# The first attention stage of a long fused kernel: its two ends reordered, and TensorE given forty transposes of the identity ahead of its first scores

## The chip, the cores and the metric

The kernel runs on one core of one Trainium2 chip. The metric is the device time of one launch in microseconds, as the median of several runs. The engines are called by their short names: PE (TensorE), DVE (VectorE), ACT (ScalarE), POOL (GpSimd) and SP (SyncE, which here only issues DMAs).

## The reference, cut to what matters

Four layers follow each other, each of the form `x = x + layernorm(f(layernorm(x)))` on eight batches of 512 x 512 float32:

```
x = x + _layernorm(_L0_attn_ref(_layernorm(x)))            # this case: its start and its end
x = x + _layernorm(_L0_ffn_ref(_layernorm(x), factors, bias))   # one matrix, the sum of 8 factors
x = x + _layernorm(_L1_attn_ref(_layernorm(x), ...))       # 8 heads, 2 groups
x = x + _layernorm(_L1_ffn_ref(_layernorm(x), ...))        # gated, 1408 wide

def _L0_attn_ref(x):
    scores = jnp.einsum('bci,bcj->bij', x, x)
    weights = jax.nn.softmax(scores, axis=-1)
    return jnp.einsum('bij,bcj->bci', weights, x)
```

The input of the kernel also holds `x_t`, the input turned, from which the context's right operand comes.

## The kernel before

**Precision.** Every float32 operand of a product is split into a high part (`xh`, `xth`, `pth`: the value written as fp32r) and a low part (`xl`, `xtl`, `ptl`: what is left), and a product is three matmuls: high by high, low by high, high by low. So the 512 x 512 scores of a batch take, for each of four row tiles `t`, three matmuls for each of four `k`. The scores are symmetric: row tile `t` computes only its columns from `t` on, and gets the rest by transposing what earlier tiles left (`copy_upper` on ACT puts it into `upper`, PE turns it back in line 901).

**The stage.** `attention_and_map` holds the first attention layer and, interleaved behind it, the first map. Each engine has its own instruction list, written out by hand for batches 0 to 7 (`written_out(body)`), and semaphores tie the lists together; within an engine the order is the order of the list, so an instruction that waits holds all behind it. For one batch:

- SP loads `x` (1 MB) and `x_t` in two halves (`load_half`, which waits until DVE has made the low parts of the batch before); for batch 0 the four tiles of `x` come in four DMAs.
- DVE takes row statistics (`tile_stats`, line 616; aggregated in 623 or 631), POOL turns them into `rs` and `shift` (`first_scales`, `scales_of`, the helper `row_scales` in lines 104 to 109), ACT writes the high part `xh` (`hi_of_xn`, line 444), POOL writes `x_scaled = x * rs` (`scaled_x`, line 315), and DVE writes the low part `xl = x_scaled + shift - xh` (`lo_of_xn`, line 637). For batch 0 this is done in two halves of two tiles.
- PE makes the scores (`scores`, line 907) in two PSUM banks; DVE takes the maximum (`maximum`, 650), ACT the exponential (`exp`, 455), DVE the inverse of the row sum (`inverse`, 655), POOL the division (`probabilities`, 320), PE turns the result (`turn`, 917), ACT and DVE split it (`hi_of_prob` 468, `lo_of_prob` 660), and PE makes the contexts (`contexts`, line 58) from it and `xth`, `xtl` (464, 643). The contexts of batch b-1 lie between the scores of batch b.
- DVE takes the contexts' statistics (`output_stats`, 665), POOL the scales (`output_scales`), ACT the normalization (`norm`, 476), and POOL adds to `x` (`add`, 336).
- POOL also issues the DMAs that sum the eight factors of the next layer's matrix (`add_factor`, 343), each waiting until the one before it has landed.

**Where scores wait.** Before the first tile of any batch but 0, PE waits for all four tiles of `xh` and `xl` of that batch; for batch 0 it waits tile by tile, one `k` at a time:

```
if t == 0 and not first:
    pe.wait_ge(xh_ready, (b + 1) * T)
    pe.wait_ge(xl_ready, (b + 1) * T)
...
    if first and t == 0:
        pe.wait_ge(xl_ready, k + 1)
```

**The end of the stage.** In the last batch's list DVE has, between `lo_of_prob(7, 1)` and `inverse(7, 3)`, the four tile statistics and their aggregation of batch 1's map. After its list ACT has `norm(6, 2)` and `norm(6, 3)` and then the high parts of the map's first turned tiles (`map_hi(0, 0, t)`, line 496), which DVE needs for the low parts (`map_lo`, 697). PE's order there is `turn(7, 2)`, `turn(7, 3)`, `contexts(6, 3)`, `map_turn` 0 and 1 (line 959), `contexts(7, 0)`, `map_turn` 2, `contexts(7, 1)`, `map_turn` 3, `contexts(7, 2)`, `contexts(7, 3)`. `map_turn` 2 waits for `map_lo` 0, whose bank it takes.

Of the kernel before, what the change touches and what calls it, by code (L numbers as in the profile page):

```python
# [15 lines left out]
T = N // P  # L16
# [14 lines left out]
ALU = mybir.AluOpType  # L31
# [47 lines left out]
def written_out(body):  # L79

    for b in range(B):
        body(b, b % 2, b == 0, b == B - 1)
# [60 lines left out]
def attention_and_map(nc, s, resident, x_in, xt_in, factors, bias, x_out, attention_buffers, following):  # L143


    if True:
# [94 lines left out]
        def block_at(t):  # L241
            return slice(t * P, (t + 1) * P)
# [50 lines left out]
        def _(pool):  # L293
# [11 lines left out]
                           pool_step, b * 2 + 2).then_inc(scales, 1)  # L305

            def scaled_x(b, tiles):
                if b == 0:
                    pool.wait_ge(*((first_scaled, 1) if tiles[0] == 0 else (scales, 1)))
                elif tiles[0] == 0:  # L310
                    pool.wait_ge(scales, b + 1)
                for t in tiles:
                    if b > 0:
                        pool.wait_ge(xl_ready, (b - 1) * T + t + 1)
                    nc.gpsimd.tensor_scalar(x_scaled[:, t, :], s.x[:, b * T + t, :], rs[:, t:t + 1], 1.0,
                                            ALU.mult, ALU.mult).then_inc(scaled_ready, 1)

# [44 lines left out]

            for h in range(2):
                first_scales(h)
                scaled_x(0, (2 * h, 2 * h + 1))

            def body(b, p, first, last):
                if not last and not first:
# [67 lines left out]
        def _(act):  # L436
# [33 lines left out]
            def norm(b, t):  # L470
                act.wait_ge(oscales, b * 2 + t // 2 + 1)
                if b == B - 1 and t >= 4:
                    act.wait_ge(last_added, t - 4 + 1)
                elif b * T + t >= 4:
                    act.wait_ge(added, b * T + t - 4 + 1)
                nc.scalar.activation(normed[:, t % 4, :], context[t][:, :], ACT.Identity,
                                     bias=oshift[:, t:t + 1], scale=ors[:, t:t + 1]).then_inc(ctx_normed, 1)
# [12 lines left out]
            def map_hi(b, p, t):  # L490
                act.wait_ge(m_turn_ready, b * T + t + 1)
                if t == 0 and b == 1:
                    act.wait_ge(ctx_ready, (B - 1) * T)
                if t == 0 and b >= 2:
                    act.wait_ge(mix_ready, (b - 1) * T)
                nc.scalar.copy(m_xth[p][:, :, block_at(t)], blocks_of(m_turned[t % 2][:, :])).then_inc(m_hi_ready, 1)
# [67 lines left out]
                    hi_of_prob(b, p, 3)  # L564

            written_out(body)
            norm(B - 2, 2)
            norm(B - 2, 3)
            map_hi(0, 0, 0)
            map_hi(0, 0, 1)  # L570
            map_hi(0, 0, 2)
            map_hi(0, 0, 3)
            norm(B - 1, 0)
# [36 lines left out]
        def _(dve):  # L610
# [47 lines left out]
            def lo_of_prob(b, p, g):  # L658
                dve.wait_ge(hi_ready, b * T + g + 1)
                nc.vector.tensor_tensor(ptl[p][:, :, block_at(g)], blocks_of(turned[g % 2][:, :]),  # L660
                                        pth[p][:, :, block_at(g)].bitcast(F32), ALU.subtract).then_inc(lo_ready, 1)
# [61 lines left out]
            for h in range(2):  # L723
                tile_stats(0, 2 * h)
                tile_stats(0, 2 * h + 1)
                first_stats_of(h)
            for t in range(T):
                lo_of_xn(0, 0, t)

            def body(b, p, first, last):  # L730
                if b >= 2:
# [43 lines left out]
                    lo_of_xn(1, 1, 2)  # L775
                maximum(b, p, 3)
                lo_of_prob(b, p, 1)
                if last:
                    for t in range(T):
                        map_tile_stats(1, t)  # L780
                    map_stats(1)
                elif first:
                    lo_of_xn(1, 1, 3)
                else:
                    lo_of_xn(b + 1, 1 - p, 2)
                inverse(b, p, 3)
                if not last and not first:
                    lo_of_xn(b + 1, 1 - p, 3)
                if not first:
# [100 lines left out]
        @block.tensor  # L890
        def _(pe):
            def scores(b, p, t, first):
                if t == 0 and not first:
                    pe.wait_ge(xh_ready, (b + 1) * T)
                    pe.wait_ge(xl_ready, (b + 1) * T)
                if not (first and t < 2):
                    pe.wait_ge(exp_ready, b * T + t - 1)
                if t > 0:
                    pe.wait_ge(copied, b * (T - 1) + t)
                for r in range(t):  # L900
                    nc.tensor.transpose(score[t % 2][:, block_at(r)], upper[r][:, block_at(t - r - 1)],
                                        s.identity[:, :])
                for k in range(T):
                    if first and t == 0:
                        pe.wait_ge(xl_ready, k + 1)
                    for l, r in ((xh, xh), (xl, xh), (xh, xl)):
                        own = nc.tensor.matmul(score[t % 2][:, t * P:], l[p][:, k, block_at(t)], r[p][:, k, t * P:],  # L907
                                               start=(k == 0 and l is xh and r is xh),
                                               stop=(k == T - 1 and r is xl))
                own.then_inc(scored, 1)  # L910
# [52 lines left out]
            def mixes(b, p, t):  # L963
# [6 lines left out]
                if b > 0:  # L970
# [2 lines left out]
                         [(l[p][:, k, block_at(t)], r[:, k, :])  # L973
                          for k in range(T) for l, r in ((m_xth, mh), (m_xtl, mh), (m_xth, ml))]).then_inc(mix_ready, 1)

            written_out(body)
            map_turn(0, 0, 0)
            map_turn(0, 0, 1)
# [1533 lines left out]
```

## Time and profile before

| | us |
|---|---|
| median of 3 runs (lowest to highest) | 1439.12 (1436.91 to 1440.38) |
| the profiled execution | 1436.28 |
| its span | 1434.5 |
| PE busy in the span | 1378.0 |
| mean granted clock of PE, as a share of full speed | 0.994 |

The first attention stage is the stretch from 0 to about 197 us. A profile of an execution gives for every instruction its start and its duration, and for an engine that stood idle before it the instruction that released it. PE's matmuls are pipelined: a matmul's duration is longer than the distance to the next one, and it is the distance that counts.

### The profile page before, as it was taken

How to read it: one execution, taken by the hardware profiler on the slowest of the kernel's cores; microseconds unless marked ns; L12 is line 12 of the kernel's file. 1: busy time of each engine (PE TensorE's matmuls, PEld its weight loads, DVE VectorE, ACT ScalarE, POOL GpSimd, SP SyncE). 2: the span in 40 equal slices, each digit the busy share in tenths (PEclk: the TensorE clock that was granted, in tenths of full speed). 3: DMA queues.
4: the chain of work that ended last, by engine and by line, in shares of the span. 5: the costliest groups of instructions: out<-in, count | busy, mean ns of one | idle time of the engine just before them, and what ended most of it. 6: DMA issues, size and time to landing. Idle time of an engine off the chain costs nothing.

```text
span 1434.5 us, 20717 instructions
## 1 busy us (share of the span) xinstructions
PE 1378.0 (96%) x6864; PEld 1131.6 (79%) x6864; DVE 1008.4 (70%) x2070; ACT 797.2 (56%) x1554; POOL 739.3 (52%) x1008
## 2 busy tenths in 40 slices
PE   5999999988999999999999998899999999999996
PEld 4888877866788888888888887688888888888884
DVE  5888868978999998989899989565343342524433
ACT  4666746649787778787878787542132222213221
POOL 5788646656547464656555555553332424333241
PEclk9999999999999999999999999999999999999998
DMA  6665232341203121221212140440101001010100
GB/s 202 166 168 122 57 103 89 118 132 45 89 16 98 36 66 53 59 74 38 89 37 89 37 141 2 147 140 1 59 1 59 31 27 58 0 58 0 58 30 30
DMA packets 53516, 101.32 MB, mean 71 GB/s; under 512 B 3760, under 2 KB 4784, under 8 KB 53424
## 3 DMA queue, kind: packets, MB, share of 16 engines
q1 hardware_dynamic: 49728, 92.83, 19.5%
q0 software_dynamic: 3696, 7.34, 3.1%
q8 instruction: 49, 0.80, 0.2%
q14 instruction: 43, 0.35, 0.1%
HBM read 70.79 MB, written 25.17 MB: 67 GB/s over the span
## 4 chain that ended last, share of the span: by engine, by line
PE 78%; DVE 11%; ACT 4%; POOL 3%; issue 3%; DMA 1%; DVEq 0%; POOLq 0%; SPq 0%; ACTq 0%
PE context L1915 12%; PE score L2393 11%; PE context L2393 11%; PE context L58 7%; PE score L58 6%; PE context L2421 5%; PE turned L2421 5%; PE score L907 4%; PE turned L1951 4%; PE context L1977 3%; PE context L1979 3%; PE context L1951 2%; DVE g_neg_max L1775 1%; DVE g_ptl L1794 1%; DVE g_q L1692 1%
## 5 line engine op out<-in xcount | busy, mean ns | idle before, releaser
L1422 POOL TENSOR_SCALAR g_prob<-g_prob,g_inv_sum 128x512 f32<-128x512 f32 x256 | 178.2, 698 | 247.3 <-DVE g_inv_sum L1780 247.3
L1560 ACT ACTIVATE g_prob<-score,g_neg_max 128x512 f32<-128x512 f32 x256 | 177.4, 693 | 105.0 <-DVE g_neg_max L1775 102.1
L2169 POOL TENSOR_TENSOR f_hl<-f_hidden,f_hh 128x512 fp32r<-128x512 f32 x88 | 121.9, 1386 | 215.8 <-DVE f_hh L2302 215.8
L1775 DVE TENSOR_REDUCE g_neg_max<-score 128x1 f32<-128x512 f32 x256 | 174.2, 680 | 30.3 <-PE score L58 29.6
L2393 PE MATMUL context<-g_hth,f_w 128*128 128x512 f32 x352 | 137.7, 391 | 2.2 <-ACT f_w L2219 2.1
L2393 PE MATMUL score<-g_hth,f_w 128*128 128x512 f32 x352 | 137.8, 392 | 0.6 <-DVE g_htl L2319 0.5
L2393 PE MATMUL context<-g_htl,f_w 128*128 128x512 f32 x352 | 137.1, 390 | 0.0
L2393 PE MATMUL score<-g_htl,f_w 128*128 128x512 f32 x352 | 137.1, 390 | 0.0
L58 PE MATMUL score<-g_kh,g_q 128*128 128x512 f32 x256 | 122.9, 480 | 7.7 <-ACT g_prob L1560 5.9
L2225 ACT ACTIVATE f_silu<-score,g_bits 128x512 f32<-128x512 f32 x44 | 30.4, 690 | 176.1 <-PE score L2393 176.1
L2225 ACT ACTIVATE f_silu<-context,g_bits 128x512 f32<-128x512 f32 x44 | 30.4, 691 | 174.4 <-PE context L2393 174.4
L2293 DVE SCALAR_TENSOR_TENSOR f_hidden<-score,g_bits,f_silu 128x512 f32<-128x512 f32 x44 | 33.0, 750 | 131.3 <-PE score L2393 131.3
L2293 DVE SCALAR_TENSOR_TENSOR f_hidden<-context,g_bits,f_silu 128x512 f32<-128x512 f32 x44 | 33.0, 749 | 128.5 <-PE context L2393 128.5
L1794 DVE TENSOR_TENSOR g_ptl<-turned,g_pth 128x512 fp32r<-128x512 f32 x171 | 115.9, 678 | 10.3 <-ACT g_pth L1607 8.9
L1607 ACT CAST g_pth<-turned 128x512 fp32r<-128x512 f32 x171 | 100.0, 585 | 12.2 <-PE turned L1951 10.5
L1951 PE MATMUL turned<-identity,g_prob 128*128 128x128 f32 x684 | 102.3, 272 | 4.0 <-POOL g_prob L1422 3.9
L1977 PE MATMUL context<-g_pth,g_v 128*128 128x512 f32 x256 | 101.3, 396 | 3.0 <-DVE g_out_sum L1728 2.8
L1951 PEld LDWEIGHTS turned<-identity,g_prob 128*128 128x128 f32 x684 | 84.1, 140 | 25.2 <-POOL g_prob L1422 5.3
L58 PE MATMUL score<-g_kl,g_q 128*128 128x512 f32 x256 | 100.9, 394 | 0.0
L1979 PE MATMUL context<-g_ptl,g_v 128*128 128x512 f32 x256 | 100.7, 393 | 0.0
L2393 PEld LDWEIGHTS context<-g_hth,f_w 128*128 128x128 f32 x352 | 66.1, 188 | 17.8 <-ACT f_w L2219 2.5
L2393 PEld LDWEIGHTS score<-g_hth,f_w 128*128 128x128 f32 x352 | 66.1, 188 | 16.2 <-DVE g_htl L2319 2.3
(261 smaller groups left out, 3941.7 us busy)
## 6 DMA issues: line engine op xcount, KB each, us to landing
xt<-x_t SPq DMA_DIRECT2D x16, 512.0 KB, 5.9
x_mixed<-x_resident SPq DMA_DIRECT2D x8, 1024.0 KB, 4.8
x_pair<-x_mixed SPq DMA_DIRECT2D x8, 1024.0 KB, 7.6
g_res<-x_mixed SPq DMA_DIRECT2D x8, 1024.0 KB, 6.2
x_attended<-g_res SPq DMA_DIRECT2D x8, 1024.0 KB, 5.1
x_pair<-x_attended SPq DMA_DIRECT2D x8, 1024.0 KB, 5.6
x_resident<-x SPq DMA_DIRECT2D x7, 1024.0 KB, 10.0
factor_sum<-factors POOLq DMA_DIRECT2D x7, 1024.0 KB, 10.9
```

Of the source, the lines that this page charges most:

```text
L58: last = nc.tensor.matmul(out, lhsT, rhs, start=(n == 0), stop=(n == len(pairs) - 1))
L1422: nc.gpsimd.tensor_scalar(prob[:, at, :], prob[:, at, :], inv_sum[:, at:at + 1], 1.0, ALU.mult, ALU.mult).then_inc(prob_ready, 1)
L1560: nc.scalar.activation(prob[:, at, :], score[u % 2][:, :], ACT.Exp, bias=neg_max[:, at:at + 1], scale=1.0, accum_out=row_sum[:, at:at + 1] ...
L1775: nc.vector.reduce_max(neg_max[:, at:at + 1], score[u % 2][:, :], AX, negate=True).then_inc(max_ready, 1)
L1794: nc.vector.tensor_tensor(ptl[:, at, :, cols], blocks_of(turned[(g - TURN_LAG) % 3][:, :]), pth[:, at, :, cols].bitcast(F32), ALU.subtract ...
L1915: last = nc.tensor.matmul(out[:, :], *pairs[n], start=(k == 0 and n == 0), stop=(k == T - 1 and n == 2))
L1951: mm = nc.tensor.transpose(turned[(g - TURN_LAG) % 3][:, cols], prob[:, turn_u % 4, cols], s.identity[:, :])
L1977: nc.tensor.matmul(output[:, :], lhsT, pth[:, hd % 2, t, :], start=(t == 0), stop=False)
L1979: mm = nc.tensor.matmul(output[:, :], lhsT, ptl[:, hd % 2, t, :], start=False, stop=(t == T - 1))
L2169: self.nc.gpsimd.tensor_tensor(self.hl[:, at, :], self.hidden[:, at, :], self.hh[:, at, :].bitcast(F32), ALU.subtract).then_inc(self.hl_re ...
L2393: last = self.nc.tensor.matmul(self.inner[pair_at(p, i) + j][:, :], lhsT, rhs, start=(k == 0 and n == 0), stop=(k == T - 1 and n == len(pa ...
L2421: last = self.nc.tensor.matmul(self.down[t][:, :], l, r, start=(i == 0 and n == 0), stop=(i == IT - 1 and n == len(halves) - 1))
```

## The change

In batch 0 the multiplication `x * rs` goes from POOL to DVE, half by half in front of the low parts. PE's wait for the inputs of a batch's first scores goes tile by tile for every batch. At the end of the stage DVE takes `inverse(7, 3)` ahead of the map statistics, and ACT takes `map_hi` 0 and 1 ahead of `norm(6, 2)` and `norm(6, 3)`. PE's list begins with forty transposes of the identity into the PSUM bank `context[3]`, which nothing reads until `contexts(0, 3)` has written it.

```diff
--- before.py
+++ after.py
@@ -305,13 +305,10 @@
                            pool_step, b * 2 + 2).then_inc(scales, 1)
 
             def scaled_x(b, tiles):
-                if b == 0:
-                    pool.wait_ge(*((first_scaled, 1) if tiles[0] == 0 else (scales, 1)))
-                elif tiles[0] == 0:
+                if tiles[0] == 0:
                     pool.wait_ge(scales, b + 1)
                 for t in tiles:
-                    if b > 0:
-                        pool.wait_ge(xl_ready, (b - 1) * T + t + 1)
+                    pool.wait_ge(xl_ready, (b - 1) * T + t + 1)
                     nc.gpsimd.tensor_scalar(x_scaled[:, t, :], s.x[:, b * T + t, :], rs[:, t:t + 1], 1.0,
                                             ALU.mult, ALU.mult).then_inc(scaled_ready, 1)
 
@@ -362,7 +359,6 @@
 
             for h in range(2):
                 first_scales(h)
-                scaled_x(0, (2 * h, 2 * h + 1))
 
             def body(b, p, first, last):
                 if not last and not first:
@@ -564,10 +560,10 @@
                     hi_of_prob(b, p, 3)
 
             written_out(body)
+            map_hi(0, 0, 0)
+            map_hi(0, 0, 1)
             norm(B - 2, 2)
             norm(B - 2, 3)
-            map_hi(0, 0, 0)
-            map_hi(0, 0, 1)
             map_hi(0, 0, 2)
             map_hi(0, 0, 3)
             norm(B - 1, 0)
@@ -724,8 +720,16 @@
                 tile_stats(0, 2 * h)
                 tile_stats(0, 2 * h + 1)
                 first_stats_of(h)
-            for t in range(T):
-                lo_of_xn(0, 0, t)
+            def first_scaled_x(h):
+                dve.wait_ge(*((first_scaled, 1) if h == 0 else (scales, 1)))
+                for t in (2 * h, 2 * h + 1):
+                    nc.vector.tensor_scalar(x_scaled[:, t, :], s.x[:, t, :], rs[:, t:t + 1], 1.0,
+                                            ALU.mult, ALU.mult).then_inc(scaled_ready, 1)
+
+            for h in range(2):
+                first_scaled_x(h)
+                lo_of_xn(0, 0, 2 * h)
+                lo_of_xn(0, 0, 2 * h + 1)
 
             def body(b, p, first, last):
                 if b >= 2:
@@ -775,15 +779,15 @@
                     lo_of_xn(1, 1, 2)
                 maximum(b, p, 3)
                 lo_of_prob(b, p, 1)
+                if first:
+                    lo_of_xn(1, 1, 3)
+                elif not last:
+                    lo_of_xn(b + 1, 1 - p, 2)
+                inverse(b, p, 3)
                 if last:
                     for t in range(T):
                         map_tile_stats(1, t)
                     map_stats(1)
-                elif first:
-                    lo_of_xn(1, 1, 3)
-                else:
-                    lo_of_xn(b + 1, 1 - p, 2)
-                inverse(b, p, 3)
                 if not last and not first:
                     lo_of_xn(b + 1, 1 - p, 3)
                 if not first:
@@ -890,9 +894,6 @@
         @block.tensor
         def _(pe):
             def scores(b, p, t, first):
-                if t == 0 and not first:
-                    pe.wait_ge(xh_ready, (b + 1) * T)
-                    pe.wait_ge(xl_ready, (b + 1) * T)
                 if not (first and t < 2):
                     pe.wait_ge(exp_ready, b * T + t - 1)
                 if t > 0:
@@ -901,8 +902,8 @@
                     nc.tensor.transpose(score[t % 2][:, block_at(r)], upper[r][:, block_at(t - r - 1)],
                                         s.identity[:, :])
                 for k in range(T):
-                    if first and t == 0:
-                        pe.wait_ge(xl_ready, k + 1)
+                    if t == 0:
+                        pe.wait_ge(xl_ready, b * T + k + 1)
                     for l, r in ((xh, xh), (xl, xh), (xh, xl)):
                         own = nc.tensor.matmul(score[t % 2][:, t * P:], l[p][:, k, block_at(t)], r[p][:, k, t * P:],
                                                start=(k == 0 and l is xh and r is xh),
@@ -973,6 +974,8 @@
                          [(l[p][:, k, block_at(t)], r[:, k, :])
                           for k in range(T) for l, r in ((m_xth, mh), (m_xtl, mh), (m_xth, ml))]).then_inc(mix_ready, 1)
 
+            for i in range(40):
+                nc.tensor.transpose(context[3][:, block_at(i % T)], s.identity[:, :], s.identity[:, :])
             written_out(body)
             map_turn(0, 0, 0)
             map_turn(0, 0, 1)
```

## Rows read from the trace of the kernel before

**Rows 1.** The page: busy time of PE, its share of the span, instructions.

```profile
PE 1378.0 (96%) x6864; PEld 1131.6 (79%) x6864; DVE 1008.4 (70%) x2070; ACT 797.2 (56%) x1554; POOL 739.3 (52%) x1008
```

**Rows 2.** Windows: stretch, length, busy PE, PEld, DVE, ACT, POOL, granted clock, DMA.

```profile
25.00:30.00 5.00, 1.45 (x6) 1.13 (x7) 4.64 (x9) 4.09 (x10) 3.86 (x4) 0.75 0.43 96
30.00:35.00 5.00, 5.00 (x18) 3.85 (x17) 2.17 (x4) 1.07 (x4) 0.85 (x1) 0.57 1.10 211
```

**Rows 3.** Waits of PE from 0 to 320 us: total, times, longest.

```profile
PE score L907 <- DVE xl L637: 11.3, 2, 10.1
PE score L907 <- issue: 3.5, 1, 3.5
PE turned L917 <- POOL prob L320: 1.9, 1, 1.9
...
PE score L959 <- DVE xl L697: 1.7, 1, 1.7
```

**Rows 4.** Timeline, 8 to 18 us: start, duration of all, engine, line, instruction.

```profile
8.18 1.37 POOL L315 TENSOR_SCALAR x_scaled<-x_resident,rs 128x512 f32<-128x512 f32 x2
8.42 0.25 DVE L623 BATCH_NORM_AGGREGATE mv<-bn 128x2 f32<-128x6 f32 x2
...
12.23 1.52 ACT L444 ACTIVATE xh<-x_resident,shift,rs 128x512 fp32r<-128x512 f32 x2 [2.61 <-POOL shift L109]
...
13.15 1.72 DVE L637 SCALAR_TENSOR_TENSOR xl<-x_scaled,shift,xh 128x512 fp32r<-128x512 f32 x2 [2.41 <-ACT xh L444]
...
14.69 1.14 ACT L464 CAST xth<-xt 128x512 fp32r<-128x512 f32 x2 [0.93 <-DMA xt<-x_t]
...
17.23 0.48 ACT L449 COPY upper<-score 128x384 f32<-128x384 f32 x1 [1.40 <-PE score L907]
```

**Rows 5.** The chain of waits, 0 to 240 us: start, length, engine, line.

```profile
14.27 2.94 PE score L907 x6
...
29.09 5.41 PE score L907 x12
...
52.97 2.76 PE score L907 x12
```

**Rows 6.** Groups of DVE: busy us, mean ns of one, idle before.

```profile
L2302 DVE CAST f_hh<-f_hidden 128x512 fp32r<-128x512 f32 x88 | 38.1, 433 | 15.2 <-PE turned L2421 6.4 <-DVE f_hidden L2293 0.9
```

**Rows 7.** Timeline, 174 to 188 us, the end of the stage.

```profile
175.15 2.47 DVE L683 BATCH_NORM_STATS2 m_bn<-x_resident 128x6 f32<-128x512 f32 x4
...
178.66 2.52 DVE L643 TENSOR_TENSOR xtl<-xt,xth 128x512 fp32r<-128x512 f32 x2
181.10 1.27 DVE L660 TENSOR_TENSOR ptl<-turned,pth 128x512 fp32r<-128x512 f32 x2
...
178.24 0.70 POOL L320 TENSOR_SCALAR prob<-prob,inv_sum 128x512 f32<-128x512 f32 x1 [3.89 <-DVE inv_sum L655]
...
183.08 0.48 PE L58 MATMUL context<-pth,xth 128*128 128x512 f32 x1
...
186.37 1.07 ACT L496 CAST xh<-score 128x512 fp32r<-128x512 f32 x2
```

**Rows 8.** Timeline, 28 to 59 us, DVE, POOL and PE.

```profile
28.25 0.73 DVE L637 SCALAR_TENSOR_TENSOR xl<-x_scaled,shift,xh 128x512 fp32r<-128x512 f32 x1
...
29.17 1.68 POOL L320 TENSOR_SCALAR prob<-prob,inv_sum 128x512 f32<-128x512 f32 x1 [1.14 <-DVE inv_sum L655]
36.59 1.32 POOL L343 DMA_DIRECT2D factor_sum<-factors  x1 [5.73 <-DMA factor_sum<-factors]
39.17 0.69 POOL L320 TENSOR_SCALAR prob<-prob,inv_sum 128x512 f32<-128x512 f32 x1 [1.26 <-DVE inv_sum L655]
...
34.34 1.04 PE L917 MATMUL turned<-identity,prob 128*128 128x128 f32 x8
...
58.66 0.39 PE L58 MATMUL context<-pth,xth 128*128 128x512 f32 x1
...
56.82 1.29 DVE L660 TENSOR_TENSOR ptl<-turned,pth 128x512 fp32r<-128x512 f32 x2 [1.07 <-ACT pth L468]
```

## The prediction

> **What bounds the kernel now.** I read the page first: PE is busy for 1378.0 of 1434.5 us [rows 1], so what counts is where PE stands idle or runs slowly, and a cut elsewhere is worth something only if a PE wait hangs on it. The windows then give the slow places. The stretch 30 to 35 us has PE busy throughout at a granted clock of 0.57, and the stretch before it has PE busy for 1.45 of 5 us at 0.75 [rows 2]: PE stood idle, the clock fell from the upper to the lower of its two levels (2.4 and 1.2 GHz), and the work after the gap paid for it. The waits of PE in the first attention stage are four kinds that matter: 11.3 us for `xl` of batch 0 (10.1 before the first matmul, 1.2 in the middle), 3.5 us put down to "issue", 1.9 us for `prob` and 1.7 us for the map's low part [rows 3]. The 3.5 us end at 29.09, right after the fourth `xl` of batch 1 (28.25 + 0.73 = 28.98), so they are the wait for all four tiles. Otherwise PE runs through, so a saving ahead of or inside the stage should move all behind it.
>
> **Part 1, batch 0's front.** Now: DVE is free of statistics at 8.67; POOL multiplies until 9.55 and only then makes the second half's scales, which release ACT at 12.23; DVE's low parts start at 13.15; the last six matmuls of score tile 0 follow, ACT's copy starts at 17.23 [rows 4]. The six take 2.94 us from 14.27 [rows 5].
> After: DVE has two multiplications more per half. The trace has none on DVE; the nearest is its cast of a 128x512 float32 tile from one source, 433 ns [rows 6]. The bounds are that and the 0.73 us of one of its low parts (the row at 28.25 [rows 8]); I take 0.4, since one source is what the cast has too. So 8.67 + 0.8 + 0.75 gives the first `xl` at about 10.3 (now 10.1; 10.8 at the other bound). POOL, free of 1.4 us of work, starts the second scales at 8.77 and needs between 1.8 us (alone) and 2.6 us (9.63 to 12.23, beside DVE's low parts): 10.6 to 11.4, and I take 11.0. Then 0.8 + 1.4 us on DVE: last `xl` at 13.3, tile 0 finished at 14.2 at the upper clock, 15.7 at the lower.
> But ACT's list has the casts of `xt` ahead of the copy. They wait for a DMA until 14.69 and end at 15.83 [rows 4], and nothing here moves that DMA. So the copy comes at 15.8 instead of 17.23: **1.4 us**, with up to 1.6 us of work ahead of it hidden. DVE has the four statistics of batch 1 (2.5 us, as for the like row of [rows 7]) ready by 16.1, in time for the maximum.
>
> **Part 2, forty transposes.** PE sits idle until 10.1, and the list starts near 2. In the trace eight transposes take 1.04 us at the upper clock, 0.11 each in sequence [rows 8]. At the lower clock the twelve matmuls of a first score tile take 5.41 us against 2.76 [rows 5], so I double: 0.22 each, 8.8 us, ending near 10.7. If the clock rises on the way they end by 9. The bounds are 0.11 (4.4 us) and 0.28 (11.2 us). At 10.7 they may hold the first matmul by 0.4 us, which the 15.8 of ACT covers. Their worth is the clock: tile 0's matmuls run at 2.94 / 6 = 0.49 us each, the lower level's pace (5.41 / 12 = 0.45), until ACT's copy. That is also hidden by ACT's 15.8, but score tile 1, now begun at 17.8 at the upper clock, would begin at 16.3, perhaps before the clock rises by itself. So the transposes insure rather than add.
> The Trainium skill (TensorE: Matmul & The Clock Gate, Part 4) says that transposes do not count as PE being busy and do not bring the full clock. No stretch of this trace consists of transposes alone, so it neither agrees nor contradicts. What that would make of the time stands among the rivals.
>
> **Part 3, batch 1's scores tile by tile.** With everything 1.4 us earlier, `xl` of batch 1 comes at about 22.9, 23.9, 25.7 and 27.5 (28.98 - 1.4, and the three before it in DVE's list). PE is free at 24.1 and follows them: three matmuls each, the last three done at 28.4. Before, the twelve ended at 34.50 (29.09 + 5.41). PE's gaps are then at most 1.2 us each, and gaps of 1.9 and 1.7 us [rows 3] left the clock alone elsewhere in the stage, so it stays up. `turn(0, 3)` needs the last `prob` of batch 0, ended at 30.85 on POOL (29.17 + 1.68), now 29.4. After it score tile 1 starts at 29.9 instead of 35.2 (34.34 + 0.87): 5.3 us earlier. The next join, `contexts(0, 0)`, needs DVE's low parts at 32.1, when PE arrives as well. **5.3 us in all so far**, of which 2.65 are the clock (5.41 - 2.76).
>
> **Part 4, what is late next.** POOL's second factor DMA waits for the first to land: it sat idle 5.73 us for it and issued at 36.59 [rows 8]. That landing moves only by the 1.4 us of Part 1, to 35.2, so POOL goes on to `prob` of batch 1 at 36.5. Without the hold it would be 39.17 - 5.3 = 33.9. So POOL, and behind it `scales_of(2)`, ACT's `xh`, and DVE's low parts, run 2.6 us behind PE. PE meets them at `contexts(1, 0)`, now at 58.66, which follows DVE's `ptl` (56.82 + 1.29 = 58.11, and 1.07 idle before it). So DVE may be 0.55 + 1.07 = 1.6 us later; it will be some 2.3 (2.6 less 0.3 idle it has on the way). PE loses 0.7. **Front: 5.3 - 0.7 = 4.6 us.** Bounds: 5.3 if the slack holds it all, 4.3 if the whole 2.6 reaches DVE. Per-tile waits help here also: batch 2's tiles come singly.
>
> **Part 5, the stage's end.** `inverse(7, 3)` goes ahead of five statistics operations: it can start at 175.2 instead of 178.0, POOL's `prob` ends at 176.1 instead of 178.94 [rows 7], and PE, through with `turn(7, 2)` only at 177.1, goes straight on: the 1.87 us are gone. PE then wants `contexts(7, 0)` at 183.08 - 1.87 = 181.2, which needs DVE's last `ptl`, ended at 182.37. DVE's list isn't shorter, it is 0.15 longer. But its two `xtl` took 2.52 us where two take 1.29 elsewhere, beside POOL's additions, which now start 2.8 us sooner and are over when the `xtl` begin. That gives 1.2 back: DVE ends at 181.2 to 182.5, and I take 181.3, a wait of 0.1 (bound 1.2).
> With `map_hi` ahead of the two norms, ACT makes it when `map_turn` is done, near 181, instead of 186.37; `map_lo` 0 is there by 183, and PE wants it at 184.2: the 1.73 us are gone. The norms wait for POOL's scales anyway, which come no later, and PE wants `norm(6, 2)` only for `contexts(7, 2)`, 3 us on. **End: 1.87 + 1.73 - 0.1 = 3.5 us** (bounds 2.4 and 3.6). From there to the map's DVE work everything hangs on `contexts(7, 3)` and moves with it; SP's loads for the next layer do too, as they wait for the same contexts.
>
> **Sum.** 4.6 + 3.5 = 8.1 us of the profiled 1436.28: 1428.2. The median of the runs shown is 1439.12, 2.8 above that execution; from the median it is **1431.0**.
>
> **Rivals.**
> *The transposes don't raise the clock.* For: nothing here shows that they do. Score tile 0 then ends at 16.0 (10.7 + 12 x 0.44), 0.2 late, and tile 1's twelve matmuls, 2.1 us at the upper clock, cost between nothing and 1.8 more, as the clock comes up. 8.1 - 0.2 - 0.9 = 7.0: 1432.1. The rule of the Trainium skill (TensorE: Matmul & The Clock Gate, Part 4) would lead here.
> *The clock falls anyway between 24 and 29 us*, PE being idle near half of it. Price up to the 2.65 us of the clock, less what PE would have waited for `turn(0, 3)` (0.6): 6.0 left, 1433.1. Against: the two gaps of nearly 2 us elsewhere.
> *The gain is given back*, because a later hold (POOL's chain of factor DMAs, or the map's DVE-bound stretch) does not move. Against: the waits behind hang on things that move. Then 0 to 2.9 us remain: 1438.
> *Slower: the transposes hold PE.* If one costs more at the lower clock than the doubling says, the first scores are late and everything with them. Up to 0.28 each nothing is lost (11.2 us after 2, then twelve at 0.22 end at 15.8). It takes 8.1 / 40 more, 0.48 each, to eat the gain, and 0.56 to be 2.9 us slower: 1442. Against: 0.56 is five times the 0.11 of the rows, where the clock only doubles.
>
> **How the numbers follow.** A difference of 0.2% (2.9 us) is about what a measurement can tell from none. Chances: forecast 0.50, no higher clock from the transposes 0.28, clock falls anyway 0.08, given back 0.09, slower 0.05. The first three are faster by over 0.2%; with a tenth of the given-back case on that side and 0.02 of the last within 0.2%, that is 0.87, 0.10 and 0.03. The range: front 5.3 and end 3.6 give 8.9, and the runs lie up to 2.2 below their median, of which I take 1.7: 1428.5. At the other side front 4.6 - 1.9 and end 2.4 leave 5.1, and 1.5 for the runs: 1435.5. That leaves out the last two cases and a little more.
>
> **What the profile after would show.** First matmul of scores at 10.3 to 10.8, and 0.22 or 0.43 us to the next; ACT's first copy at 15.8; PE's idle before batch 1's scores in pieces under 1.3 us and no granted clock below 1.00 until the end; POOL's second factor issue near 35.2; a PE wait of some 0.7 us at `contexts(1, 0)`; `turn(7, 3)` right behind `turn(7, 2)`; no wait before `map_turn` 2. The prediction is wrong if the clock column falls again near 27 us, if PE's first scores come after 13 us, or if PE waits at `contexts(7, 0)` for over 1 us.

## The result, and the profile after

The changed kernel takes 1431.41 us (median of 6 runs, 1429.95 to 1433.23), the kernel before 1439.57 (6 runs, 1436.91 to 1440.50): a ratio of 0.9946, 95% interval 0.9933 to 0.9958, or 8.2 us less. The forecast was 1431.0 with 1428.5 to 1435.5. The profiled execution of the changed kernel took 1429.95, its span is 1428.1; against the one of before that is only 6.3 us, and the reason is told below.

The page after, its rows of busy time and of the granted clock:

```profile
PE 1382.8 (97%) x6904; PEld 1136.4 (80%) x6904; DVE 1008.8 (71%) x2074; ACT 796.7 (56%) x1554; POOL 736.3 (52%) x1004
...
PEclk9999999999999999999999999999999999999998
```

PE has 4.8 us more work than in [rows 1], the forty transposes among it, and the span is 6.4 us shorter. The transposes stand in the timeline as one run, at the end of which PE waits for `xl`:

```profile
1.91 7.19 PE L978 MATMUL context<-identity 128*128 128x128 f32 x40 [1.91 <-PEq L1003]
10.21 0.50 PE L908 MATMUL score<-xh 128*128 128x512 f32 x1 [1.11 <-DVE xl L633]
```

The windows after, with the same columns as [rows 2]:

```profile
25.00:30.00 5.00, 4.22 (x23) 3.16 (x22) 4.98 (x10) 4.36 (x10) 3.68 (x3) 1.00 0.39 55
30.00:35.00 5.00, 5.00 (x29) 4.41 (x28) 4.66 (x13) 1.86 (x6) 0.00 (x0) 1.00 1.09 235
```

From 25 to 35 us PE is busy for 9.2 of 10 us at 1.00, where [rows 2] had 6.5 at 0.75 and 0.57. The waits of PE from 0 to 320 us, beside [rows 3]:

```profile
PE score L908 <- DVE xl L633: 2.3, 3, 1.1
PE score L902 <- ACT upper L445: 2.1, 3, 1.0
...
PE turned L918 <- POOL prob L317: 1.8, 3, 1.1
...
PE context L58 <- issue: 0.8, 1, 0.8
```

The 3.5 us and the 1.7 us are gone, and of the 11.3 us for `xl` 2.3 are left, mostly because the transposes now fill the idle time up to 9.10. What is left for `prob` is in the first batch (three waits, the longest 1.1), not at the stage's end. The waits for ACT's copies have grown to 2.1 us; before they were

```profile
PE score L901 <- ACT upper L449: 1.1, 2, 0.6
```

New is 0.8 us of "issue" before a context. The timeline of the front, beside [rows 4] and [rows 8]:

```profile
8.47 0.91 DVE L726 TENSOR_SCALAR x_scaled<-x_resident,rs 128x512 f32<-128x512 f32 x2 [0.43 <-POOL shift L109]
...
11.04 0.89 DVE L726 TENSOR_SCALAR x_scaled<-x_resident,rs 128x512 f32<-128x512 f32 x2 [0.20 <-POOL shift L109]
...
11.04 1.52 ACT L440 ACTIVATE xh<-x_resident,shift,rs 128x512 fp32r<-128x512 f32 x2 [1.05 <-POOL shift L109]
13.84 1.14 ACT L460 CAST xth<-xt 128x512 fp32r<-128x512 f32 x2 [1.27 <-DMA xt<-x_t]
14.88 0.47 ACT L445 COPY upper<-score 128x384 f32<-128x384 f32 x1
...
36.03 1.32 POOL L340 DMA_DIRECT2D factor_sum<-factors  x1 [7.33 <-DMA factor_sum<-factors]
...
51.46 0.30 PE L902 MATMUL score<-identity,upper 128*128 128x128 f32 x1 [0.56 <-ACT upper L445]
...
54.65 0.47 PE L58 MATMUL context<-pth,xth 128*128 128x512 f32 x1 [0.80 <-issue]
```

ACT's first copy comes at 14.88 (forecast 15.8), right behind the casts of `xt`. Of the 2.35 us that it is earlier than in [rows 4], 0.85 aren't the change's: the DMA of `xt` was issued at 7.34 in this execution and let ACT start at 13.84, where the execution of before has 8.11 and 14.69 (and the second trace of the changed kernel, below, 8.11 and 14.92). POOL waits 7.33 us for the first factor DMA and issues the second at 36.03 (forecast 35.2), and PE waits 0.80 before `contexts(1, 0)` (forecast 0.7) and 0.56 at 51.46. The end of the stage, beside [rows 7]:

```profile
174.90 1.28 DVE L639 TENSOR_TENSOR xtl<-xt,xth 128x512 fp32r<-128x512 f32 x2
176.09 1.28 DVE L656 TENSOR_TENSOR ptl<-turned,pth 128x512 fp32r<-128x512 f32 x2
...
176.99 1.08 ACT L492 CAST xh<-score 128x512 fp32r<-128x512 f32 x2 [1.61 <-PE score L960]
179.83 1.45 ACT L472 ACTIVATE normed<-context,oshift,ors 128x512 f32<-128x512 f32 x2 [1.76 <-POOL oshift L328]
...
171.63 0.70 POOL L317 TENSOR_SCALAR prob<-prob,inv_sum 128x512 f32<-128x512 f32 x1 [1.13 <-DVE inv_sum L651]
172.29 2.54 POOL L333 TENSOR_TENSOR x_resident<-x_resident,normed 128x512 f32<-128x512 f32 x2
...
172.67 1.03 PE L918 MATMUL turned<-identity,prob 128*128 128x128 f32 x8
...
176.35 1.04 PE L960 MATMUL score<-identity,x_scaled 128*128 128x128 f32 x8
...
180.32 0.60 PE L960 MATMUL score<-identity,x_scaled 128*128 128x128 f32 x4
```

The two additions of POOL stood later and took longer before:

```profile
178.90 3.44 POOL L336 TENSOR_TENSOR x_resident<-x_resident,normed 128x512 f32<-128x512 f32 x2
```

`turn(7, 2)` and `turn(7, 3)` are one run of eight transposes, `map_turn` 0 and 1 follow twelve matmuls later, ACT makes `map_hi` at 176.99 ahead of the norms at 179.83, and `map_turn` 2 has no wait.

### The profile page after: what moved, and what is told of

It is laid out like the page before. It is cut to its first block, busy times and chain, and to the rows that moved or that the text cites. A ratio compares the mean times of both kernels' runs of the same rounds, so it can differ in the third digit from the quotient of the medians.

```text
span 1428.1 us, 20797 instructions
## 1 busy us (share of the span) xinstructions
PE 1382.8 (97%) x6904; PEld 1136.4 (80%) x6904; DVE 1008.8 (71%) x2074; ACT 796.7 (56%) x1554; POOL 736.3 (52%) x1004
## 3 DMA queue, kind: packets, MB, share of 16 engines
q0 software_dynamic: 3696, 7.34, 3.1%
## 4 chain that ended last, share of the span: by engine, by line
PE 76%; DVE 11%; POOL 4%; ACT 4%; issue 3%; DMA 2%; DVEq 0%; POOLq 0%; SPq 0%; ACTq 0%
PE context L1918 12%; PE score L2396 11%; PE context L2396 11%; PE score L58 6%; PE context L58 6%; PE context L2424 5%; PE turned L2424 5%; PE turned L1954 4%; PE score L908 3%; PE context L1980 3%; PE context L1982 3%; PE context L1954 2%; DVE g_neg_max L1778 1%; DVE g_ptl L1797 1%; DVE g_q L1695 1%
```

## The experiments

Each of the twelve was timed against the kernel before on the same chip, in three groups on three chips, where the median of before was 1439.3 to 1439.9; so the ratio is what to compare. The table has the median, the ratio to before with its interval, and, from one profiled execution each, when PE starts the first matmul of `contexts(0, 0)`, `contexts(1, 0)` and `contexts(7, 1)`. The difference to the first line is what PE has won by then.

| kernel | median | ratio (95%) | contexts(0, 0) | contexts(1, 0) | contexts(7, 1) |
|---|---|---|---|---|---|
| before | 1439.57 | | 37.43 | 58.66 | 188.21 |
| after | 1431.41 | 0.9946 (0.9933 to 0.9958) | 31.48 | 54.65 | 180.67 |
| after_again | 1431.65 | 0.9951 (0.9936 to 0.9966) | 32.76 | 54.55 | 180.43 |
| a_no_turns | 1430.54 | 0.9930 (0.9916 to 0.9944) | 32.32 | 55.35 | 181.21 |
| b_old_end | 1436.87 | 0.9977 (0.9968 to 0.9986) | 32.33 | 56.70 | 187.88 |
| c_whole_wait | 1432.95 | 0.9958 (0.9944 to 0.9971) | 36.14 | 57.37 | 183.23 |
| d_factor_late | 1430.27 | 0.9930 (0.9916 to 0.9943) | 33.45 | 55.45 | 181.39 |
| e_turns_alone | 1438.15 | 0.9992 (0.9982 to 1.0003) | 37.47 | 58.70 | 188.18 |
| f_tiles_alone | 1435.91 | 0.9978 (0.9967 to 0.9988) | 33.66 | 55.16 | 184.78 |
| h_inv_alone | 1437.56 | 0.9993 (0.9983 to 1.0004) | 37.00 | 58.23 | 186.34 |
| k_pool_scaled | 1432.11 | 0.9950 (0.9937 to 0.9964) | 33.57 | 55.27 | 181.16 |
| m_turns60 | 1430.79 | 0.9944 (0.9931 to 0.9958) | 32.11 | 55.75 | 181.61 |
| n_factor_later | 1431.64 | 0.9935 (0.9921 to 0.9948) | 31.87 | 53.08 | 180.42 |
| o_later_no_turns | 1429.29 | 0.9931 (0.9917 to 0.9944) | 32.18 | 53.39 | 179.36 |

The ratios resolve some 2 us. The three time columns resolve tenths, but of one execution: between the two traces of the changed kernel `contexts(0, 0)` differs by 1.3 us, `contexts(1, 0)` by 0.1 and `contexts(7, 1)` by 0.2. Where ratio and trace differ both are told.

**The changed kernel without its transposes** (a_no_turns).

```diff
-            for i in range(40):
-                nc.tensor.transpose(context[3][:, block_at(i % T)], s.identity[:, :], s.identity[:, :])
```

> The changed kernel without the forty transposes. Theory (the start of batch 2 is set by POOL's wait for the first factor DMA, not by PE): score tile 0 runs at 0.43 us a matmul and its copy comes some 0.7 us later, PE's later stretches may be late by up to 1.8 us more, but the hold at contexts(1, 0) takes 1.9 us of whatever the front has, so the whole loses 0 to 0.7 us against the changed kernel: ratio to before about 0.995. Rival 1 (the transposes' clock is worth its full price): 2.5 us lost, ratio 0.9963. Rival 2 (without them the clock never settles before 35 us): 4 us lost, ratio 0.9973.

0.9930, no slower than the changed kernel. In the traces PE is 0.7 to 0.8 us later at `contexts(1, 0)` than in the two of the changed kernel. Both rivals fall (2.5 and 4 us lost); what the transposes give is at most those 0.7 to 0.8 us, at the edge of what the theory allowed. Against the first trace even the 0.7 is the lateness of POOL's second factor issue (36.73 for 36.03), and whether the transposes had a part in that isn't shown.

**The old end with the new front** (b_old_end): the two reorderings of the last hunks for ACT and DVE undone.

```diff
-            map_hi(0, 0, 0)
-            map_hi(0, 0, 1)
             norm(B - 2, 2)
             norm(B - 2, 3)
+            map_hi(0, 0, 0)
+            map_hi(0, 0, 1)
...
-                inverse(b, p, 3)
                 if last:
...
                     map_stats(1)
+                inverse(b, p, 3)
```

> The changed kernel with the end of the stage as before (ACT's two norms ahead of map_hi, DVE's inverse behind the map statistics): the front alone. Theory: the end is worth 3.5 us, so the ratio to before is 0.9946 + 3.5/1439.6 = 0.9970, with waits of 1.9 us for prob and 1.7 us for the map's low part back in the trace. Rival (the end's gain overlaps with something later that waits anyway): 0 to 1.5 us lost, ratio 0.9946 to 0.9957.

0.9977: 4.5 us lost, one more than the order of the work explains, though the intervals allow 3.5. The front of this execution is also poorer (1.96 us won at `contexts(1, 0)`; the first factor landed 11.7 us after its issue at 26.36). But the windows of this execution show something more, in the very stretch of the old end's waits:

```profile
175.00:177.00 2.00, 0.22 (x3) 0.00 (x0) 1.90 (x9) 1.84 (x4) 0.66 (x2) 1.00 0.00 0
177.00:181.00 4.00, 3.91 (x12) 3.28 (x13) 3.45 (x4) 0.59 (x1) 3.40 (x3) 0.57 0.00 0
181.00:183.00 2.00, 2.00 (x14) 1.75 (x13) 0.81 (x3) 0.00 (x0) 0.00 (x0) 1.00 0.00 0
```

PE idle for most of two microseconds, then the clock at 0.57: between `turn(7, 2)`, ahead of the old end's first wait, and `contexts(7, 1)` the gain falls from 1.90 to 0.33 us. In the one execution of before the same wait left the clock at 1.00.

**PE waits for all four tiles again** (c_whole_wait).

```diff
             def scores(b, p, t, first):
+                if t == 0 and not first:
+                    pe.wait_ge(xh_ready, (b + 1) * T)
+                    pe.wait_ge(xl_ready, (b + 1) * T)
...
-                    if t == 0:
-                        pe.wait_ge(xl_ready, b * T + k + 1)
+                    if first and t == 0:
+                        pe.wait_ge(xl_ready, k + 1)
```

> The changed kernel with PE waiting for all four tiles before batch 1's scores and those of later batches. PE then starts batch 1's twelve matmuls near 26.9 us and is through with score tile 1 some 1.4 us later than in the changed kernel. Theory (POOL's factor hold sets contexts(1, 0)): the 1.4 us are swallowed by the 1.9 us of hold, 0 to 0.5 us lost, ratio 0.9946 to 0.995, if the granted clock stays at 1.00. Rival 1: all 1.4 us are lost, ratio 0.9956. Rival 2: with 2.5 us of idle PE in one piece the clock falls near 25 us as it did before the change, 3 to 4 us lost, ratio 0.997.

Its windows, by which rival 2 holds for this execution:

```profile
25.00:30.00 5.00, 2.54 (x7) 2.04 (x7) 4.98 (x10) 3.43 (x7) 4.25 (x4) 0.65 0.32 33
30.00:35.00 5.00, 5.00 (x22) 4.22 (x22) 1.30 (x3) 1.56 (x3) 0.00 (x0) 0.67 1.06 216
```

The clock falls as before the change, the front's gain is 1.29 us at `contexts(1, 0)` in place of 4.0, and it stays so. The ratio, 0.9958, is a smaller loss than the trace's 2.7 us, within its interval.

**The wait tile by tile alone, on the kernel before** (f_tiles_alone): the reverse of that edit, nothing else.

```diff
-                if t == 0 and not first:
-                    pe.wait_ge(xh_ready, (b + 1) * T)
-                    pe.wait_ge(xl_ready, (b + 1) * T)
...
-                    if first and t == 0:
-                        pe.wait_ge(xl_ready, k + 1)
+                    if t == 0:
+                        pe.wait_ge(xl_ready, b * T + k + 1)
```

> The kernel before with PE's wait tile by tile for every batch, and nothing else. Theory: batch 1's scores follow xl at 25.4, 27.1 and 29.0 us, the clock stays up, PE is 3.9 us ahead at turn(0, 3), and POOL's factor hold (landing unmoved at 36.6) leaves 2.0 to 2.9 us at contexts(1, 0): ratio 0.998 to 0.9986, more than half of the front's 4.0 us. Rival 1 (the clock falls in the gaps all the same): under 1 us, ratio 0.9993 or more. Rival 2 (no hold): 3.9 us, ratio 0.9973.

0.9978, and in the trace 3.50 us won at `contexts(1, 0)` and 3.43 at `contexts(7, 1)`. That is more than the 2.0 to 2.9 expected, and most of the front's 4.0. The clock stays up where [rows 2] had it at 0.75 and 0.57:

```profile
25.00:30.00 5.00, 3.86 (x17) 2.58 (x18) 4.63 (x9) 4.09 (x9) 3.85 (x4) 1.00 0.43 86
30.00:35.00 5.00, 4.53 (x28) 4.04 (x27) 4.61 (x8) 3.08 (x8) 0.91 (x1) 1.00 1.11 210
```

POOL's hold was priced too high here: the second factor is issued at 36.48 and PE is 3.77 ahead, so little is over.

**The transposes alone, on the kernel before** (e_turns_alone).

> The kernel before with the forty transposes alone. Theory: PE's clock is up by 8 us, score tile 0's first six matmuls go by at 0.235 us each, but then PE idles from 11.5 to 14.3 us for xl; whatever is won up to there (at most 1.2 us at ACT's first copy) does not move batch 1's xl, which hangs on DVE and POOL, so the clock still falls near 27 us: 0 to 0.7 us gained, ratio 0.9995 to 1.000. Rival (the clock is what the front's gain comes from): 2 us or more, ratio 0.9986 or less.

0.9992 (0.9982 to 1.0003), and in the trace nothing is won from 14.28 us on. Its windows:

```profile
10.00:14.00 4.00, 1.66 (x6) 1.01 (x6) 1.60 (x3) 1.52 (x2) 3.36 (x7) 1.00 0.98 354
14.00:17.00 3.00, 2.72 (x6) 1.82 (x6) 3.00 (x6) 1.14 (x2) 0.00 (x0) 0.50 1.00 378
...
25.00:30.00 5.00, 1.45 (x6) 1.13 (x7) 4.64 (x9) 4.10 (x10) 3.86 (x4) 0.76 0.38 94
30.00:35.00 5.00, 5.00 (x17) 3.89 (x16) 2.17 (x4) 1.02 (x3) 0.85 (x1) 0.55 1.09 208
```

The clock that the transposes raised is lost at 14.0 us and again at 27.6, because PE waits for `xl` all the same.

**DVE's inverse alone, on the kernel before** (h_inv_alone).

```diff
                 lo_of_prob(b, p, 1)
+                inverse(b, p, 3)
                 if last:
...
                     map_stats(1)
...
-                inverse(b, p, 3)
```

> The kernel before with DVE's inverse(7, 3) ahead of the map statistics, and nothing else. Theory: PE's wait of 1.9 us for prob goes, contexts(7, 0) waits 0 to 0.2 us for DVE's last ptl, and the 1.7 us wait at map_turn 2 stays: 1.7 to 1.9 us gained, ratio 0.9987 to 0.9988. Rival 1 (contexts(7, 0) waits for DVE by 1.2 us): 0.7 us, ratio 0.9995. Rival 2 (PE's two idle stretches also cost it the clock in some executions, which one alone does not): the median gains more than the profile's order explains, 2.5 us or more.

0.9993 (0.9983 to 1.0004), too wide to tell 0.7 from 1.8 us. The trace tells: PE has won 0.52 us by 170 us (its front happened to be that much ahead) and 1.87 at `contexts(7, 1)`, so 1.4 us, less than the 1.7 to 1.9 expected. The gain was 2.62 at `contexts(6, 3)`; 0.34 went at `contexts(7, 0)`, and 0.41 as the wait for the map's low part grew from 1.7 to 2.1. The two reorderings of the end belong together: 1.4 alone, 3.7 in pair. (ACT's reordering alone was not run.)

**The multiplication back on POOL** (k_pool_scaled).

```diff
                 first_scales(h)
+                scaled_x(0, (2 * h, 2 * h + 1))
...
-            for h in range(2):
-                first_scaled_x(h)
-                lo_of_xn(0, 0, 2 * h)
-                lo_of_xn(0, 0, 2 * h + 1)
+            for t in range(T):
+                lo_of_xn(0, 0, t)
```

> The changed kernel with batch 0's multiplication back on POOL, the rest of the change kept. Theory: batch 1's tile-by-tile wait alone gave 3.4 us of front and the end 3.7 us; the move to DVE and the transposes add 0.5 us at batch 2, so 0.3 to 0.7 us are lost: ratio 0.995 to 0.9955, ACT's first copy near 16 to 16.5 us. Rival (the move is worth the 1.4 us that it gives ACT's first copy): 1.4 us lost at 80 us and ratio 0.9958 or more.

0.9950. `contexts(1, 0)` starts 0.6 to 0.7 us later than in the changed kernel, ACT's copy at 15.93. The theory holds. The way runs through POOL: it issues the first factor DMA at 26.48 (25.49 and 25.66 in the changed kernel), and the second at 36.65 (36.03 and 35.37). This execution's clock also dipped, from 15.8 to 19.2 us, though the front doesn't show it: its gain at `contexts(0, 0)`, 3.86 us, is that of f_tiles_alone (3.77), which had no such dip.

**Sixty transposes** (m_turns60), `range(60)` for `range(40)`.

> The changed kernel with sixty transposes in place of forty. Theory: the idle PE between the end of the transposes (7.4 to 9.1 us) and the first scores at 10.2 us is filled, the first scores are held by at most 1.2 us, which ACT's copy covers, and the clock cannot dip at 11 us as it did in one execution; the median stays within 0.5 us of the changed kernel: ratio 0.9945 to 0.995. Rival (PE held by the transposes sets the front): the gain at 80 us falls below 3.0 us, ratio 0.9955.

0.9944, as expected. PE runs them from 1.91 to 10.39 without holding the scores (first at 10.14, behind them by overlap). The trace's gain at 80 us is 2.8, which the rival named, but the scores are on time (`contexts(0, 0)` at 32.11); what is late is the factor DMA (second issue at 37.13, 1.1 later than in the changed kernel). So the cause that the rival gives isn't there.

**POOL's second factor DMA a little later** (d_factor_late), and **later still** (n_factor_later).

```diff
-                if not last and not first:
+                if not last and b > 1:
                     add_factor(b + 1)
...
                 elif not first:
                     scales_of(b + 1)
+                if b == 1:                      # d_factor_late
+                    add_factor(2)
...
                 elif not last:
                     scaled_x(b + 1, (0, 1, 2))
+                if b == 1:                      # n_factor_later
+                    add_factor(2)
```

Each kernel has one of the two added calls, and both have the first line changed.

> The changed kernel with POOL's second factor DMA issued behind prob 0 and the scales of batch 2 in place of ahead of them. Theory: POOL's hold of 7.3 us no longer stands ahead of batch 1's work, prob 0 of batch 1 comes near 33 us in place of 37, PE's waits at 51 and 54 us go, and 1.9 us are gained: ratio to before 0.9933. Rival (DVE or ACT holds contexts(1, 0) by itself, or the later factor DMAs are late in turn): within 0.4 us of the changed kernel, ratio 0.9946.

> The changed kernel with POOL's second factor DMA issued behind the first three multiplications for batch 2, where the version above that moved it less far still had its 1.3 us of issue ahead of them. Theory (the hold before contexts(1, 0) is POOL's: its wait and its issue): the gain of PE at 35 us and at 80 us is the same within 0.4 us, where it fell by 2.1 us in the first trace of the changed kernel; ratio 0.9935 to 0.994. Rival (DVE has too much between 45 and 55 us whatever POOL does): the gain still falls by 0.9 us or more, ratio 0.9945.

d_factor_late: 0.9930, but its trace doesn't answer. The clock dipped in it from 11.7 to 18.5 us (0.50 from 12 to 16 us), transposes or not, and PE still lost 0.77 us between `contexts(0, 0)` and `contexts(1, 0)`, since POOL's 1.3 us of issue stood ahead of the multiplications. n_factor_later's timeline of POOL:

```profile
33.48 0.69 POOL L317 TENSOR_SCALAR prob<-prob,inv_sum 128x512 f32<-128x512 f32 x1 [4.35 <-DVE inv_sum L653]
...
36.66 0.70 POOL L317 TENSOR_SCALAR prob<-prob,inv_sum 128x512 f32<-128x512 f32 x1
...
39.76 1.33 POOL L340 DMA_DIRECT2D factor_sum<-factors  x1
...
50.43 1.33 POOL L340 DMA_DIRECT2D factor_sum<-factors  x1 [5.75 <-DMA factor_sum<-factors]
```

POOL makes `prob` of batch 1 at 33.48 and 36.66 (after: 36.88 and 40.28), and PE loses nothing: 5.56 us won at `contexts(0, 0)`, 5.58 at `contexts(1, 0)`, against 5.95 and 4.01 in the changed kernel. The hold was POOL's. But the third factor's DMA now waits 5.75 us for the second, and by batch 3 (80 us) the gain is down to 4.11. The ratio, 0.9935, isn't separable from the changed kernel's.

**The same without transposes** (o_later_no_turns).

> The same without the forty transposes, as the candidate for the best version. Theory: the transposes' clock is worth 0 to 0.7 us once nothing swallows the front, so 0 to 0.7 us behind the version with them, both ahead of the changed kernel: ratio 0.9935 to 0.9945. Rival (the transposes cost something elsewhere, as the run without them hinted at 0.993): 1 us or more faster than with them.

The best of the lot: 1429.29 us, 0.9931 (0.9917 to 0.9944), with 5.1 us of the front kept to 80 us (the second factor landed 1.3 us sooner after its issue than in n_factor_later) and 8.85 at `contexts(7, 1)`. Against n_factor_later, the version with the transposes, PE is 0.3 us later at `contexts(1, 0)`, as the theory says; by the medians it is 2.3 us faster, which is the rival's figure, but the ratios (0.9931 and 0.9935) don't separate the two. It is the candidate for the best version, and 2 us below the changed kernel by the medians; the intervals overlap.

**The changed kernel again** (after_again).

> The changed kernel itself, beside the three below on one chip. Ratio to before 0.9946 again, within 0.001. Theory on single executions (where the granted clock dips depends on the execution): PE's own order and waits are the same in this trace as in the first one of this kernel, but the dips of the clock column lie at other places, and the front's gain at contexts(1, 0) differs by up to 1 us. Rival: the dips are a property of the kernel and lie at 335 us again.

0.9951. The first high entry of the clock column lies at 7.8 us in place of 7.3, and PE is 4.11 us ahead at `contexts(1, 0)` in place of 4.01, after 4.67 in place of 5.95 at `contexts(0, 0)`: in this execution the DMA of `xt` landed 1.1 us later (14.92 for 13.84) and ACT's copy is at 15.96, while the first factor landed 0.7 us sooner. There is no dip at 335 us; it lies at 885 us. So the theory holds and the rival falls.

## Why the prediction was right

**Part 1 (1.4 us at ACT's copy).** Right in kind: the copy stands right behind the casts of `xt`, at 14.88 and 15.96 in the two traces, and the DMA sets it. The multiplications took 0.91 us a pair (0.8 taken), the second scales released ACT at 11.04 and 11.64 (11.0 taken). What the working took as fixed, the start of those casts, was 13.84 and 14.92 against 14.69 before, so PE was 2.36 us ahead behind the copy in one execution and 1.27 in the other. With the DMA's part taken out, 1.5 us are left in both, for the 1.4. At batch 2 the move is worth 0.6 to 0.7 us by k_pool_scaled, as the later hold takes the rest.

**Part 2 (transposes insure rather than add).** They do raise the clock: the nine traces of the eight kernels with them have the first high entry between 4.9 and 7.8 us, the five others between 13.2 and 18.0. The rival that they don't (0.28) is out. That they add little stands: a_no_turns, e_turns_alone and o_later_no_turns show at most 0.8 us in traces and nothing clear of the intervals in the ratios. At the lower clock one took 0.21 us (0.22 in the working), and the run ended at 9.10 (by 9 in the working).

**Part 3 (5.3 us at score tile 1 of batch 1).** Measured 5.95 and 4.67. It holds most of the front: 3.5 us by f_tiles_alone, 2.7 by c_whole_wait. The clock's fall goes with it: the four traces in which PE waits for all four tiles (before, c_whole_wait, e_turns_alone, h_inv_alone) have a fall between 26.5 and 27.6 us, and the ten with the wait tile by tile have none there. How much of the 5.3 is the clock (2.65 in the working) and how much the earlier start no run separates.

**Part 4 (a hold of 0.7 us; front 4.6).** The mechanism is shown by n_factor_later. The size was off: 1.9 us in one execution, 0.6 in the other; front 4.0 and 4.1 for 4.6. Nor was it all at `contexts(1, 0)`: of the 1.9 us in the first trace 0.3 went at 41.03 (`turn(1, 1)`), 0.7 at 51.46 (the transposes of ACT's copy, in the scores of batch 2) and 0.9 at 54.65. The working let the landing move by as much as the issue; it moved from 36.59 to 36.03 with an issue 1.05 us sooner, so the transfer itself took longer (10.5 us for 10.1), and PE was further ahead than 5.3. In the other trace it landed at 35.37 (35.2 in the working) and PE was 4.67 ahead, and the hold came near the 0.7. The traces show the hold more closely than the working had it: in six of them (after, a_no_turns, b_old_end, f_tiles_alone, k_pool_scaled, m_turns60) `contexts(1, 0)` starts 18.6 to 18.7 us behind POOL's second factor issue, though that issue lies anywhere from 36.03 to 38.06. (19.2 in after_again; 20.4 in c_whole_wait, where PE isn't far enough ahead to be held.) So where PE is far enough ahead, a later landing costs its whole lateness, whatever PE had won before.

**Part 5 (3.5 us).** Measured 3.69 in one trace and 3.70 in the other (from `turn(7, 2)` to `contexts(7, 1)`: 3.85 to 7.54, 4.08 to 7.78), 0.1 above the two waits' sum. The parts differ a little from the working's: 2.09 us at the first wait (1.87), 0.33 lost at `contexts(7, 0)` (0.1), 1.93 at the second (1.73). DVE's `xtl` went back to 1.28 us for two and POOL's additions to 2.54 from 3.44, as the working had it; the last `ptl` ended at 177.37 and `contexts(7, 0)` started at 177.47, so that is the wait of Part 5, at three times its size.

**The sum.** In the traces the stage gives 7.5 and 7.8 us for 8.1. Behind it the order of the work gives back little (0.2 us of PE's gain between 895 and 900 us in the first trace, where no clock dipped); what differs is the clock. The forecast named no granted clock below 1.00 until the end, and that did not come true. In the changed kernel's trace it dips at 335 us, in a stretch where PE waits for ACT's `g_prob`:

```profile
330.00:335.00 5.00, 3.10 (x20) 2.18 (x19) 4.26 (x10) 4.21 (x11) 1.38 (x2) 1.00 0.00 0
335.00:340.00 5.00, 5.00 (x21) 4.06 (x20) 4.01 (x10) 3.74 (x9) 1.69 (x3) 0.66 0.01 3
340.00:345.00 5.00, 4.49 (x28) 3.34 (x27) 3.79 (x9) 4.40 (x12) 2.94 (x4) 1.00 0.00 0
```

PE's gain there goes from 7.6 to 6.6 us, and is 6.3 at the end. The execution of before had no dip behind its first, and its 1436.28 lies 3.3 below its median. That is why the two profiled executions differ by less than the medians. How much of the medians' 8.2 is the stage and how much fewer dips stays open, but the record shows that dips have a part. The mean granted clock of 53 executions of the kernel before has the median 0.990, that of the changed kernel's twelve 0.994. The fall of [rows 2] lasts 6.8 us at half the clock, which takes 0.0024 off the mean (an estimate from the column and the span); the rest of the 0.004 lies elsewhere, and the traces have their other dips almost all behind the stage.

So the nearness of 1431.0 to 1431.41 is in part luck. The two ends are worth 7.5 and 7.8 us in the traces for the 8.1 of the working, whose front was 0.5 to 0.6 us too high and whose end was 0.2 too low, and the 2.8 us from the profiled execution to the median were carried over as if later dips were the same before and after.

## What to carry to other kernels

A wait for all pieces ahead of work that takes them one by one is worth looking for first: here it alone was worth 3.4 us in the trace. Part of that is likely the clock that fell in the gap and no longer does; no run separates the part. A gain ahead of a fixed transfer is kept only as far as the transfer's consumer has slack; look for the next engine that sits idle for a DMA (5.73 us in [rows 8]) and what stands behind it in its list. Two waits close together should be removed together, as the second takes over part of the first. With differences of a fifth of a per cent, follow the start of one and the same instruction through the traces.

## What the hardware showed that I had not expected

Transposes do bring the clock up. The windows of the changed kernel from 4 to 9 us (the clock column reads 1.00 ahead of its first entry, so the rise has to be read from the pace):

```profile
4.00:7.00 3.00, 3.00 (x16) 3.00 (x15) 2.02 (x5) 0.00 (x0) 0.32 (x2) 1.00 0.78 281
7.00:8.00 1.00, 1.00 (x10) 1.00 (x9) 0.97 (x4) 0.00 (x0) 0.85 (x3) 1.00 0.04 4
8.00:9.00 1.00, 1.00 (x11) 0.86 (x8) 0.57 (x3) 0.53 (x1) 0.84 (x4) 1.00 0.54 150
```

A count takes in the transposes that a window cuts; by their starts in the trace they are 0.21 us apart up to 7.27 us and 0.11 from 7.41 on, and the scores behind them run at 0.23 us to the next where they took 0.43. The Trainium skill (TensorE: Matmul & The Clock Gate, Part 4) says that the full clock doesn't engage for transposes, which don't count as PE being busy in the same way. The traces don't agree, and the measurement decides: in all nine of the kernels with transposes the clock rose while PE had run nothing but these (4.9 to 7.8 us), and in the five without it rose at 13.2 to 18.0.

And where the clock dips differs from execution to execution of one kernel: the changed kernel's two traces have it at 335 and at 885 us, at waits that both have. Behind the stage the fourteen traces have dips at four places only, from 309 to 314, 334 to 339, 884 to 892 and 914 to 922 us, none of them in the trace of before and four in that of f_tiles_alone. An idle stretch doesn't settle it by its length: PE idles for 3.28 us before 892.87 in the trace of before, with the clock up throughout, and the dip at 335 us stands at a wait of 1.22. b_old_end lost 1.6 us to one at 177 us, and between 860 and 940 us it lost another 3.1 us against the execution of before.

That such dips make up much of the 3 to 4 us by which the runs of one kernel spread isn't shown instruction by instruction, as the other executions have no trace, but their mean granted clock is on record and goes with the time. Of the 53 executions of before, the 38 with 0.989 or 0.990 took 1438.6 to 1441.6 us, and the four with 0.994 took 1435.6 to 1436.5. The profiled execution of before is of the second kind, so a working from its trace starts from a kernel that is better than its median.
